# Loads issued ahead of the block border, and the last expert tile by tile, in a two-layer macaron network on one core

## The reference

```
x = x + 0.5 * L0_ffn(ln(x))      # 8 experts, top 2, capacity 256, hidden 512, tanh gelu
x = x + L0_attn(ln(x))           # 16 heads of 8, keys and values from a strided convolution
x = x + 0.5 * L0_ffn(ln(x))
x = x + 0.5 * L1_ffn(ln(x))      # ln, causal attention, ln, 16 experts, top 2, capacity 512
x = x + L1_attn(ln(x))           # causal attention
x = x + 0.5 * L1_ffn(ln(x))
return x
```

## Time and profile before

| | us |
|---|---|
| median of three runs | 1981.46 |
| fastest and slowest of them | 1974.45, 1981.49 |
| span of the profiled execution | 1903.6 |
| its own time | not on the page, which has the span alone |
| PE busy | 1565.1 (82%) |
| DVE busy | 1298.9 (68%) |
| ACT busy | 964.7 (51%) |
| POOL busy | 1076.0 (57%) |

### The profile page before, as it was taken

How to read it: one execution, slowest core, us unless ns; L and a number is a source line. 1 busy time by engine, 2 the same in 40 slices (tenths; PEclk the granted TensorE clock), 3 DMA queues, 4 the chain that set the end, 5 groups by cost and what they waited for, 6 DMA issues and landing times. The chain is left out here.

```text
span 1903.6 us, 46256 instructions
## 1 busy us (share of the span) xinstructions
PE 1565.1 (82%) x17646; PEld 967.9 (51%) x17646; DVE 1298.9 (68%) x3322; ACT 964.7 (51%) x2039; POOL 1076.0 (57%) x1712
## 2 busy tenths in 40 slices
PE   5648788885499999984897799999999999973992
PEld 5522333345355555553675355555555555552772
DVE  7348888774678878876321778888888878874224
ACT  4215667642156676650332266667777776631331
POOL 3447766414477856576354466455566675663552
PEclk9967999977689999985898599999999999975996
DMA  8443323203433322210442432232233233112445
GB/s 295 123 125 95 102 67 98 77 24 101 130 101 114 92 81 78 81 40 28 139 144 88 147 107 78 80 109 87 78 104 94 78 95 94 46 34 66 148 125 160
DMA packets 233185, 188.08 MB, mean 99 GB/s; under 512 B 30044, under 2 KB 221368, under 8 KB 232326
## 3 DMA queue, kind: packets, MB, share of 16 engines
q1 hardware_dynamic: 222582, 166.36, 29.2%
q0 software_dynamic: 10240, 18.76, 3.0%
q10 hardware_dynamic: 144, 0.00, 0.0%
HBM read 104.34 MB, written 80.74 MB: 97 GB/s over the span
## 5 line engine op out<-in xcount | busy, mean ns | idle before, releaser
L988 DVE TENSOR_REDUCE mx<-PS 128x2 f32<-128x512 f32 (+3 forms) x1408 | 784.4, 612 | 193.9 <-PE PS L648 149.2
L838 ACT ACTIVATE pt<-PS 128x512 f32<-128x512 f32 (+2 forms) x1408 | 662.9, 537 | 297.4 <-PE PS L648 233.3
L664 PE MATMUL PS<-ka,qa 52*128 52x256 bf16 (+3 forms) x2048 | 482.0, 307 | 56.3 <-DVE mx L988 39.8
L773 PE MATMUL PS<-qa,ka 55*128 55x512 bf16 (+3 forms) x1792 | 466.1, 321 | 17.8 <-DMA qa<-nm 16.5
L718 PE MATMUL PS<-pt,vs 128*32 128x512 f32 (+3 forms) x3584 | 346.0, 479 | 0.7 <-ACT pt L838 0.7
L648 PE MATMUL PS<-mask_q,identh 64*128 64x64 bf16 x3072 | 314.7, 192 | 0.0
L648 PE MATMUL PS<-mask_k,identh 64*128 64x64 bf16 x3072 | 307.1, 191 | 0.0
L773 PEld LDWEIGHTS PS<-qa,ka 55*128 55x128 bf16 x1792 | 166.7, 94 | 250.2 <-issue 119.3
L648 PEld LDWEIGHTS PS<-mask_k,identh 64*128 64x128 bf16 x3072 | 249.7, 96 | 49.0 <-issue 3.3
L648 PEld LDWEIGHTS PS<-mask_q,identh 64*128 64x128 bf16 x3072 | 258.2, 98 | 31.1 <-issue 6.3
L1141 POOL CAST nm<-nm 16x128 bf16<-16x128 f32 x128 | 36.0, 281 | 352.4 <-ACT nm L870 338.3
(11 more groups left out here) (249 smaller groups left out, 2327.3 us busy)
## 6 DMA issues: line engine op xcount, KB each, us to landing
pt<-in_f_w SPq DMA_DIRECT2D x96, 256.0 KB, 3.2
qa<-q_parts SPq DMA_DIRECT2D x256, 96.0 KB, 2.3
ka<-k_parts SPq DMA_DIRECT2D x192, 96.0 KB, 2.3
q_parts<-parts SPq DMA_DIRECT2D x32, 384.0 KB, 2.9
k_parts<-parts SPq DMA_DIRECT2D x24, 384.0 KB, 2.6
xn<-y_rows SPq DMA_DIRECT2D x32, 256.0 KB, 3.3
hid<-y_rows SPq DMA_DIRECT2D x32, 256.0 KB, 3.5
q_parts<-parts SPq DMA_DIRECT2D x32, 256.0 KB, 3.1
```

The lines of the kernel that those rows point to most:

```text
L664: mm = pe.matmul(PS[:, bank, i * n:(i + 1) * n], k.qa[rows, b % 2, g, h // 2, qb * P:(qb + 1) * P], k.ka[rows, b % 2, g, h // 2, 0:n], sta ...
L773: mm = pe.matmul(PS[:, bank, i * n:(i + 1) * n], k.ka[rows, b % 2, g, h // 2, kb * P:(kb + 1) * P], k.qa[rows, b % 2, g, h // 2, q0:S], st ...
L838: nc.scalar.activation(k.pt[:, u % 2, at[c]:at[c] + len(heads) * n], PS[:, SC_BANK + c % RING, 0:len(heads) * n], ACT.Exp, scale=SCORE_SCA ...
L988: nc.vector.tensor_reduce(out, PS[:, MX_BANK + t % RING, 0:len(heads) * n] .rearrange("p (h n) -> p h n", n=n), AX.X, ALU.max).then_inc(s. ...
```

## The change

- In the 16-expert stages the weights of experts 0 and 1 and the rows of experts 0, 1 and 2 are no longer loaded at the start of `moe`. SP issues them at the end of the `attention` block: the weights after `pv_done` and `inv_full`, the rows after all sends have landed.
- At the end of `moe` SP loads `results` results, not one: four (eight DMAs) ahead of each attention, all eight (sixteen DMAs) ahead of the closing block. The loads at the start of `attention` and in the closing block are gone.
- The last expert of every `moe` is computed tile by tile: `last_output` has the tiles outside and the quarters inside, waits for all four gelus first, and puts each tile in a bank of its own; `last_result` adds the bias tile by tile; `deliver` waits before each tile of the last expert.

```diff
@@ end of attention, SP @@
-            for i in range(1, B - 4):
-                load_results(sp, k, i)
...
+            else:
+                sp.wait_ge(*s.pv_done.at(U))
+                sp.wait_ge(*s.inv_full.at(1))
+                for e in range(2):
+                    load_weights(sp, k, front, e)
+                sp.wait_ge(*s.first_sent.at(16 * NT))
+                for j, (first, end) in enumerate(r.phases):
+                    sp.wait_ge(*s.second_sent[j].at(16 * (end - first)))
+                for e in range(AHEAD):
+                    load_rows(sp, k, r, e)
@@ moe, PE @@
+    LAST_BANKS = (Y_BANK + (E - 1) % 2, XT_BANK, Y_BANK + E % 2, XT_BANK + 1)
+            def last_output():
+                par = (E - 1) % 2
+                pe.wait_ge(*s.w2_landed[par].at(16 * PAIRS))
+                pe.wait_ge(*s.y_ready.at(E - 2))
+                pe.wait_ge(*s.act_done.at(E * FC))
+                for t in range(ST):
+                    if t == 2:
+                        pe.wait_ge(*s.y_ready.at(E - 1))
+                    for f in range(FC):
+                        mm = pe.matmul(PS[:, LAST_BANKS[t], 0:C], k.hT[:, par, f, t * P:(t + 1) * P],
+                                       k.w2[:, par, f, :], start=(f == 0), stop=(f == FC - 1))
+                    mm.then_inc(s.y_full.h, 1)
@@ moe, DVE @@
+            def last_result():
+                ring = (E - 1) % RING_E
+                dve.wait_ge(*s.y_stored[ring].at(16 * ST * (E // RING_E - 1)))
+                for t in range(ST):
+                    dve.wait_ge(*s.y_full.at(E + t))
+                    nc.vector.tensor_tensor(k.ys[ring][:, t, :], PS[:, LAST_BANKS[t], 0:C], w.b2[:, (E - 1) * C:E * C],
+                                            ALU.add).then_inc(s.y_ready.h, 1)
@@ moe, POOL, deliver @@
-                pool.wait_ge(*s.y_ready.at(e + 1))
                 for t in range(ST):
                     n = e * ST + t
+                    if t == 0 or e == E - 1:
+                        pool.wait_ge(*s.y_ready.at(e + 1 + t))
@@ moe, SP @@
-            if r.sent:
-                for e in range(AHEAD):
-                    fetch_sent(e)
-                    if e < 2:
-                        load_weights(e // 2, e % 2)
...
             for ring in range(RING_E):
                 sp.wait_ge(*s.y_stored[ring].at(16 * ST * (E // RING_E)))
-            load_results(sp, k, 0)
+            for i in range(results):
+                load_results(sp, k, i)
@@ program @@
-        experts1(route1)
+        experts1(route1, B - 4)
         attention(nc, k, [entry1, entry1f], route1)
-        experts1(route1)
+        experts1(route1, B)
@@ closing block, SP @@
-                for i in range(1, B):
-                    load_results(sp, k, i)
```

More of the change, by code:

```diff
@@ L68 @@
 INV_BANK = 5
+AHEAD = 3
 FIRST_PHASES = ((0, 16), (16, 32))
@@ L1323, in attention, with load_weights, load_rows, moe @@
         signal.base += n
-def moe(nc, k, r, src, dst, gate_scale, renorm, src_scale):
+def load_weights(sp, k, w, e):
+    s, par = k.sig, e % 2
+    sp.dma_start(k.w1[:, par, :], w.w1[e * C:(e + 1) * C, :]).then_inc(s.w1_landed[par].h, 16)
+    sp.dma_start(k.w2[:, par, :, :], w.w2[e * FH:(e + 1) * FH, :].rearrange("(f p) c -> p f c", p=P))\
+        .then_inc(s.w2_landed[par].h, 16)
+def load_rows(sp, k, r, e):
+    ring, capacity = e % RING_E, r.w.capacity
+    sp.dma_start(k.xe[ring][:, :, :], k.xe_rows[e * capacity:(e + 1) * capacity, :]
+                 .rearrange("(t p) c -> p t c", p=P)).then_inc(k.sig.xe_loaded[ring].h, 16)
+def moe(nc, k, r, src, dst, gate_scale, renorm, src_scale, results):
     s, PS, w, E, capacity = k.sig, k.PS, r.w, r.E, r.w.capacity
@@ L1339, in over_e @@
         return ap.unsqueeze(2).to_broadcast([P, NT, E])
-    AHEAD = RING_E - 1
+    LAST_BANKS = (Y_BANK + (E - 1) % 2, XT_BANK, Y_BANK + E % 2, XT_BANK + 1)
     landed, landings = (s.xe_loaded, 16) if r.sent else (s.xe_landed, 16 * ST)
@@ L1386, in _ @@
                     rows_T(e + 1)
-                output(e)
+                    output(e)
+            last_output()
         @block.scalar
@@ L1483, in _ @@
                     scale_source(e - 1)
-            result(E - 1)
+            last_result()
             k.route_steps = link.n
@@ L1519, in _ @@
         def _(sp):
-            def load_weights(j, par):
-                e = 2 * j + par
-                if not (isinstance(j, int) and j < 1):
+            for e in range(E):
+                if e >= 2:
                     sp.wait_ge(*s.y_full.at(e - 1))
[L1524 to L1537, removed]
-            if r.sent:
-                for e in range(AHEAD):
-                    fetch_sent(e)
-                    if e < 2:
-                        load_weights(e // 2, e % 2)
-            for e in range(E):
                 if not (r.sent and e < 2):
-                    load_weights(e // 2, e % 2)
+                    load_weights(sp, k, w, e)
                 if r.sent and e + AHEAD < E:
-                    fetch_sent(e + AHEAD)
+                    if e >= 1:
+                        sp.wait_ge(*s.eT_full.at(e))
+                    load_rows(sp, k, r, e + AHEAD)
             for ring in range(RING_E):
                 sp.wait_ge(*s.y_stored[ring].at(16 * ST * (E // RING_E)))
-            load_results(sp, k, 0)
+            for i in range(results):
+                load_results(sp, k, i)
     counts = {
         s.diff_ready: 2, s.exp_ready: 2, s.rt_step: k.route_steps, s.eT_full: E, s.eT_free: E,
-        s.h_full: FC * E, s.act_done: FC * E, s.y_full: E, s.y_ready: E,
+        s.h_full: FC * E, s.act_done: FC * E, s.y_full: E + ST - 1, s.y_ready: E + ST - 1,
     }
@@ L1947, in experts0, with experts1 @@
         def experts0(r):
-            moe(nc, k, r, x, x, 0.5, ("add", 1e-9), 0.0)
-        def experts1(r):
-            moe(nc, k, r, hid, x, 0.5 * 0.8, ("max", 1.1920929e-07), 0.5)
+            moe(nc, k, r, x, x, 0.5, ("add", 1e-9), 0.0, B - 4)
+        def experts1(r, results):
+            moe(nc, k, r, hid, x, 0.5 * 0.8, ("max", 1.1920929e-07), 0.5, results)
         entry0 = Segment(attn0, x, x, False)
```

## The result

The change made the kernel **slower by 0.85%**: 1997.18 us (median of four runs, 1995.21 to 1998.76) against 1980.28 us for the kernel before (four runs, 1974.45 to 1981.49). The ratio is 1.0085, with an interval of 1.0067 to 1.0102, so +13.3 to +20.2 us. That lies outside the stated range of 1974 to 1990.

The account below looks back on a forecast made before the run. The prediction took block borders as the bound, held by POOL's drain or, after the change, SP's issues. Terms -5.7, +1.3, +1.3, -0.6 and +5.0 summed to +1.3 us, giving 1982.8 us, no change, range 1974 to 1990.

Parts of the forecast that it names:

- I make the sum against the span and carry the difference over to the median.: Whole kernel: the 77.9 us between span 1903.6 and median 1981.46 lie outside the span, untouched by the change.
- Weights and rows ahead of the border: Entry into both 16-expert stages: PE can start when DVE does, 2.81 and 2.90 us gained, -5.7 us in sum.
- PE within 0.2 us of DVE: Sign at both 16-expert stages: PE's first transposes come within 0.2 us of DVE's first instruction.
- Last expert tile by tile: End of expert stages: SP wakes 1.9 us earlier after each 16-expert stage, 0.4 (0 to 0.7) after 8-expert ones.
- The three later tiles come 0.93 apart, faster than POOL's 1.27: Last expert of a 16-expert stage: tiles after the first arrive every 0.93 us, quicker than POOL's 1.27 per scatter.
- a later scatter must end at least 1.5 us earlier: Error sign: a stage's last scatter ends less than 1.5 us earlier against the last gelu than before's 8.6 us.
- Eight loads ahead of each attention: Borders before the three attentions: SP's eight issues take 5.06 us and hold the border, +1.3, +1.3 and -0.6 us.
- Sixteen loads ahead of the last border: Closing block: SP issues for 12.4 us before DVE starts, then 17.9 us without waits, +5.0 us (bounds +1.2, +7.8).
- One (short issues): Rival for the loads ahead of borders: every issue takes 0.54 us, sum -4.8, 1976.7 us; chance 0.14.
- Two (weights collide with the sends): Rival at 16-expert entries: early weights delay POOL's sends up to 3.5 us each, 1989.8, at worst 1992.6; chance 0.09.
- Three (the border doesn't wait for SP): Rival at attention and last borders: POOL's drain alone holds them, sum -12.0, 1969.5 us, faster; chance 0.06.
- Four (tiles gain nothing): Rival for the last expert: added waits cost POOL what the early tile brings, +4.6, 1987.4 us; chance 0.11.

Follow-up runs that it names:

- before again: The kernel before, unchanged, run and profiled a second time: 1979.54 us, ratio 0.9992, profile span 1983.5 us.
- experiment 2: Kernel before with only the early loads of weights and rows ahead of the two 16-expert stages: 1982.21 us, ratio 1.0005.
- Experiment 5: Kernel before with only the early loads for the 16-expert stages, each expert's rows issued ahead of its weights: 1974.80 us, ratio 0.9977.
- experiment 12: Kernel before with the last expert tile by tile on PE and DVE, POOL waiting for all four tiles before its last scatters: 1982.41 us, ratio 1.0007.
- experiments 6 to 8: Kernel before with only the last `moe` loading more results ahead of the last border, 8, 5 and 3: ratios 1.0031, 1.0005 and 0.9986.
- experiment 6: Kernel before with only all eight results loaded ahead of the last border: ratio 1.0031.
- experiment 8: Kernel before with only three results loaded ahead of the last border, five behind it: ratio 0.9986.

## Why the prediction was wrong

The loads of results were forecast at +7.0 and came out at +12.0 by the offsets; the early weights and rows were forecast at -5.7 and came out at +2.1. Either miss alone would have left the time near or inside the range; together they made it slower.

**"I make the sum against the span and carry the difference over to the median."** This is the step that failed first. The 77.9 us between span and median were not outside the span: they are stretches of standing still inside the blocks in which POOL issues indirect DMAs, and the timed executions have them. They moved the very place that the first term rests on. They fall among POOL's sends and hold up PE, DVE and ACT, while POOL goes on: its first send now starts 140 us before the occupants are read, not 89. So the last send ends 1.8 us before the occupants are read, not 11.9 us behind. The row "its own time: not on the page" should have been a warning that two numbers 4% apart can't belong to one execution without a cause.

**Weights and rows ahead of the border: -5.7 forecast, +2.1 by the offsets of the change (+1.0 measured alone).** Three things failed in it. The cover was gone: in before again only 3.8 us are left from the reading until the border opens behind POOL's drain, not 17.5. And the rows were priced at the 2.8 us that PE waited for them before, although four weight loads (1 MB, 3.5 us at the 301 GB/s of the earlier trace rows) now stood ahead of them on SP's queue. In the forecast they had long landed; here they had not, and PE had the rows 5.0 to 5.8 us behind their issue (experiment 2 and the change). Experiment 5 shows this step by itself: with the rows first the gain is -4.6, near the 5.7 and from both stages, though by 2.2 to 2.3 each and not by 2.8 to 2.9. The rest is the third thing: the forecast had SP at the border 2 us ahead of POOL; in the change and in experiments 2 and 5 SP comes last, 0.3 to 0.9 us behind POOL. The prediction named PE within 0.2 us of DVE as its sign; with the change PE starts 3.4 and 3.7 us behind DVE.

The Trainium skill (DMA: Bandwidth & Descriptors, "Two DMAs through the same engine are not ordered") says that within one queue of a DMA engine descriptors start in order, though they needn't finish so. The landings of experiment 2 and the 5.5 us between experiments 2 and 5 agree.

**Last expert tile by tile: 1.9 of SP's waking forecast at the long stages, 0.45 measured alone, 0.4 and 1.0 in the change.** The first tile was right: POOL starts 1.95 behind the gelu against 3.85 before. "The three later tiles come 0.93 apart, faster than POOL's 1.27" was wrong. The third comes 2.3 us late while POOL issues (experiment 12). The bound that a later scatter must end at least 1.5 us earlier, named as a sign of error, was broken: 7.6 against 8.6. At the short stages the gain was 0.05, inside the stated 0 to 0.7, and 0.4 was taken.

**Eight loads ahead of each attention: +1.3, +1.3, -0.6 forecast, +2.0, +2.1, +1.4 measured.** The mechanism was right: SP's list holds the border, and eight issues are what it adds. The eight took 5.4 and 5.6 us, against 5.06. The rest is the waking: 0.35 at the first two and some 1.45 at the third are the tiles' missing gain. 0.35 + 0.35 makes the first two, 0.53 + 1.45 the third, each to 0.1.

**Sixteen loads ahead of the last border: +5.0 forecast, +6.5 measured.** Sixteen issues took 12.8 us (12.4 forecast), 0.46 from the last of them to DVE (0.45), then 17.9 us of combines without a wait (17.9). The missing 1.5 are the 1.0 of the waking (9.0 instead of 8.0 behind the gelu), the 0.4 of the issues, and rounding. This was the largest single loss, and its mechanism and size were read right from the earlier trace rows.

**The rivals.** One (short issues) is out: the sixth issue and those behind it took 0.65 to 1.29 us. Here the page of the Trainium skill that calls the initiating time usually small (same page, "Issuing engines are not separate DMA queues") doesn't hold for sixteen loads of 256 KB in a row ahead of a border. Two (weights collide with the sends) was not put to the test, since the last send ends some 2 us before the first weight load is issued; POOL's drain there takes 12.4 us with the change and without it. Three (the border doesn't wait for SP) is out by experiments 6 to 8. Four (tiles gain nothing) came nearly true, at a quarter of the forecast gain at the long stages alone (a third in the change), through a path that it didn't name. The rival that happened was missing: that the weights delay the rows, which cost the first term and not only its cover.

**The sum.** By the offsets of one profile each: +2.1 (two entries), +5.5 (three attentions), +6.5 (last border) make +14.1, against +16.9 between the medians (13.3 to 20.2). The remaining 2.8 us lie within the interval and are not located. A block in which nothing was changed differs by as much between single profiles (the first attention has 328.6 us before again and 323.6 in experiment 6), so they can't say more.

## What to carry to other kernels

Before a sum is made, hold the span of the profile against the timed runs; if they differ by more than a per cent, the profile shows another execution than the one to be predicted, and every "who comes last" in it is open. A load moved ahead of a barrier is only free while the issuing engine's last issue stays ahead of whoever holds the barrier: here, by the offsets, six issues were free, ten cost 1.7 us and sixteen 7.2. On one queue, put what the next block's first instruction waits for ahead of what is needed later; that order alone was worth 5.5 us.

## What the runs showed of the hardware

*Standing still beside indirect DMAs.* In every profile but the one shown first, and so, by their length, in the timed runs too, PE, DVE and ACT stop for mostly 2 to 7 us at a time while POOL issues indirect DMAs, with no semaphore that would explain it. In the kernel after, in the second attention:

```profile
871.89 0.97 POOL L416 DMA_INDIRECT xe_rows<-xn,slot  x1 [0.30 <-issue]
872.42 0.38 ACT L839 ACTIVATE pt<-PS 128x256 f32<-128x256 f32 x1 [4.39 <-remote]
...
872.86 0.61 PE L774 MATMUL PS<-qa,ka 55*128 55x512 bf16 x1 [3.99 <-issue]
...
873.16 0.97 POOL L416 DMA_INDIRECT xe_rows<-xn,slot  x1 [0.30 <-issue]
```

POOL goes on issuing at its pace of 1.27 us through the gap. The DMA engines are mostly idle in it: from 868 to 873 they move 128 packets, 0.25 MB, all of the sends' own queue, so neither other loads nor the loading of instructions fills the gap. In before again all 37 gaps of this kind above 2 us have POOL's indirect DMAs beside them, but the 64 scatters of each 16-expert stage bring none. The same program, profiled first, had no such stretch. Why one execution has them and another not stays open; experiment 12 shows the link with POOL's DMAs at one tile only.

*POOL's drain.* Behind its last indirect DMA POOL's drain runs on: 5.3 us after the last row send (1818.94 to 1824.2, before again) and after the fourth scatter of an expert, 2.7 us where an expert has two. Spreading the four scatters over the tiles didn't shorten it. In the kernel before this holds the border, and it is the cover under which the three results of experiment 8 and the first rows of experiment 5 are issued.

*Issues in a row.* Loads of 256 KB that SP issues back to back take 0.51 us each at first and 0.8 us from about the seventh on, with single ones between 1.0 and 1.6.
